# Four graph layers on one core: a first LSTM turn with orders of its own, and its loads rearranged

## The reference

```
h = relu(adj @ (x @ Wg0 + bg0))
h = relu(adj @ (h @ Wg1 + bg1))
for p in 1, 2, 3, 4:          # windows of p rows
    wins = h[:, :nw*p].reshape(B*nw, p, H)
    last = lstm_last(Wih[p-1], Whh[p-1], bih[p-1], bhh[p-1], wins)   # gates i, f, g, o
    h[:, p-1::p] = last       # the last row of each window is replaced
```

## Time and profile before

| what | us |
|---|---|
| median of 3 runs | 1201.16 (1200.19 to 1201.65) |
| the profiled execution | 1202.18 |
| its span | 1200.4 |
| PE busy | 1161.4 (97%) |
| DVE busy | 991.0 (83%) |
| ACT busy | 817.9 (68%) |
| POOL busy | 387.9 (32%) |

### The profile page before, as it was taken

One profiled execution on the slowest core, in us unless ns is written; L12 is line 12 of the kernel. 1 busy time (PEld: TensorE's weight loads), 2 busy tenths in 40 slices (PEclk: granted clock), 3 DMA queues, 4 the chain that ended last, 5 costly groups with the idle time before them and its releaser, 6 DMA issues. The chain is left out here.

```text
span 1200.4 us, 23784 instructions
## 1 busy us (share of the span) xinstructions
PE 1161.4 (97%) x7820; PEld 1021.9 (85%) x7820; DVE 991.0 (83%) x2791; ACT 817.9 (68%) x1826; POOL 387.9 (32%) x717
## 2 busy tenths in 40 slices
PE   5999999999999999999998999989999999999998
PEld 4798898998988989889897898877777798889997
DVE  5888988888889888898886899988877689976665
ACT  4685886868868768588685777757777777753332
POOL 4211100100001001010011677756666487742332
PEclk9999999999999999999998999999999999999999
DMA  9400000000000000000000000000000000002222
GB/s 261 121 1 1 1 2 0 0 0 0 0 0 0 0 0 0 0 0 0 1 1 1 2 2 2 2 1 1 2 1 1 1 2 1 2 3 69 71 69 73
DMA packets 26306, 20.85 MB, mean 17 GB/s; under 512 B 1776, under 2 KB 22256, under 8 KB 26224
## 3 DMA queue, kind: packets, MB, share of 16 engines
q1 hardware_dynamic: 25648, 19.68, 5.8%
q10 hardware_dynamic: 576, 0.13, 0.1%
HBM read 11.42 MB, written 8.39 MB: 17 GB/s over the span
## 5 line engine op out<-in xcount | busy, mean ns | idle before, releaser
L554 ACT ACTIVATE gate<-ps,b_lstm 128x256 f32<-128x256 f32 (+2 forms) x624 | 309.5, 564 | 94.4 <-PE ps L581 92.9
L579 PE MATMUL ps<-H_hi,w_hi 128*128 128x256 f32 (+2 forms) x624 | 210.3, 338 | 1.9 <-DVE H_lo L470 1.2
L580 PE MATMUL ps<-H_hi,w_lo 128*128 128x256 f32 (+2 forms) x624 | 205.1, 330 | 0.0
L581 PE MATMUL ps<-H_lo,w_hi 128*128 128x256 f32 (+2 forms) x624 | 193.2, 330 | 0.0
L131 POOL TENSOR_SCALAR rstd<-mv 128x8 f32<-128x8 f32 x16 | 5.0, 311 | 500.3 <-DVE mv L111 500.1
L579 PEld LDWEIGHTS ps<-H_hi,w_hi 128*128 128x128 f32 x624 | 117.7, 189 | 15.8 <-DVE H_lo L470 3.2
L580 PEld LDWEIGHTS ps<-H_hi,w_lo 128*128 128x128 f32 x624 | 117.9, 189 | 8.1
L581 PEld LDWEIGHTS ps<-H_lo,w_hi 128*128 128x128 f32 x624 | 115.4, 189 | 10.1 <-DVE H_lo L508 1.5
L579 PE MATMUL ps<-hid_hi,w_hi 128*128 128x256 f32 (+2 forms) x384 | 120.5, 320 | 0.3
L580 PE MATMUL ps<-hid_hi,w_lo 128*128 128x256 f32 (+2 forms) x384 | 116.8, 311 | 0.0
L561 ACT ACTIVATE tanh_c<-cell 128x512 f32<-128x512 f32 (+2 forms) x176 | 90.9, 516 | 24.5 <-DVE cell L498 17.4
(11 more groups left out here) (205 smaller groups left out, 3095.6 us busy)
## 6 DMA issues: line engine op xcount, KB each, us to landing
out<-x SPq DMA_DIRECT2D x32, 256.0 KB, 2.3
x<-in_WihT SPq DMA_DIRECT2D x1, 768.0 KB, 11.3
x<-in_WhhT SPq DMA_DIRECT2D x1, 768.0 KB, 6.0
x<-in_x_in SPq DMA_DIRECT2D x2, 256.0 KB, 3.6
x<-in_x_in SPq DMA_DIRECT2D x1, 512.0 KB, 7.9
x<-in_WihT SPq DMA_DIRECT2D x1, 256.0 KB, 8.2
tanh_c<-in_WqkvT SPq DMA_DIRECT2D x1, 192.0 KB, 5.0
w_sb<-in_W SPq DMA_DIRECT2D x1, 192.0 KB, 4.2
```

What stands on the lines that cost most here:

```text
L554: nc.scalar.activation(gate[:, g, z, 0:w * GB], gate_bank(g, k, m)[:, 0:w * GB], ACT.Tanh if z == G else ACT.Sigmoid, bias=b_lstm[:, 4 * ( ...
L579: nc.tensor.matmul(dst, w_hi[:, src, p - 1, z], v_hi, start=start, stop=False)
L580: return nc.tensor.matmul(dst, w_lo[:, src, p - 1, z], v_hi, start=False, stop=False)
L581: return nc.tensor.matmul(dst, w_hi[:, src, p - 1, z], v_lo, start=False, stop=stop)
```

## The change

The first turn gets orders of its own (FIRST_TENSOR, FIRST_VECTOR, FIRST_SCALAR). In them a letter x stands for the next item of a list of preparations of that engine, so that preparation can stand anywhere. The function `merged` runs the first order, then turns 1 to 7 as before.

- **Norm.** Statistics come in four quarters (SUMS 0 to 3), each with the addition of epsilon on DVE; POOL does the power only; DVE multiplies (SHIFT). ACT normalizes batch by batch, and PE waits for each batch of A0, not for four.
- **Loads.** Group 1 of x comes in two halves, directly behind group 0; the graph weights and the second bias are issued from ACT's queue, the edge lists and the LSTM biases from SP's behind x. SP then waits for the last quarter of the first 16 batches and issues the two 768 KB loads, and only then the second 16 batches of x.
- **Scratch.** Keys, edge rows and the attention operands move to a part of x that is loaded last but two; that load waits until they are taken.
- **Weights.** ACT splits weights 0 to 2 before its first A1 part, the other four and `w2` between gates later on. POOL makes the `w_lo` before `adj_causal`.
- **PSUM.** The sorting product and the fused weights both use bank 7; the fused one waits for the gate that reads this bank, and steps 1 and 2 of group 1 wait until they are taken.

```diff
+        PREPARE_TENSOR = [(COLUMN_SUM, 0), (BIAS_SUM, 0), (SORTED, 0), (FUSED, 0)]
+        PREPARE_VECTOR = [(SUMS, 0), (BIAS, 0), (SUMS, 1), (SHIFT, 0), (SUMS, 2), (SHIFT, 1), (SUMS, 3), (SHIFT, 2),
+                          (SHIFT, 3), (ADDEND, 0), (KEYS, 0), (LSTM_BIAS, 0), (RANK, 0), (RANK, 1), (MOVE, 0), (MOVE, 1),
+                          (DIAGONAL, 0), (TAKE_SORTED, 0), (TAKE_FUSED, 0)]
+        PREPARE_SCALAR = ([(NORM, j) for j in range(NB)] + [(SPLIT, n) for n in range(len(SPLITS))] + [(SPLIT2, 0)])
+
+
+        FIRST_TENSOR = ("xxaaaaabbabbaabbaaabbaaabbxbbbbaaxaaaaaaaabbabbbbbaaabbbbaaaaaaaaabaabbbbbabaaabbbabbbbbaaababb"
+                        "baaaaaaaaaabbabbbbbaaaabbbaaababbabaabbbbab")
+        FIRST_VECTOR = ("xxxxxxxxxxaxaxxxaabbxaabbxxattbbaaaxbaabbbaxtaabtbtaasbasabbasttaabbttbsbaassbaabsbsaabbaabbasa"
+                        "abbbbaabaabbaaabbabbaabbabb")
+        FIRST_SCALAR = ("xxxxxxxxaxaxxxxxxxbbxxxaaaaabbaxaaabbabbbbaaaabbxaaabbaabbaaaabbbbbaaaaxbbabxbaaabbbaabbaaaabbb"
+                        "babaaassbbabbsxaaatatabbbssbbssaaasbbbtbaabttttt")
...
+            for z in first_order:
+                if z == "x":
+                    prepare(*next(firsts[z]))
+                else:
+                    do(0, int(z in "bt"), *next(firsts[z]), False)
...
-                for to, s in ((w_g[:, 0], Wg0), (w_g[:, 1], Wg1), (b1_bc[:], bg1.to_broadcast([P, P]))):
-                    sp.dma_start(to, s).then_inc(S["ld_g"], 16)
-                sp.dma_start(*batches(GB, NB)).then_inc(S["ld_xb"], 16)
+                sp.dma_start(*batches(GB, GB + GB // 2)).then_inc(S["ld_xb"], 16)
+                sp.dma_start(*batches(GB + GB // 2, NB)).then_inc(S["ld_xc"], 16)
                 sp.dma_start(raw_all[0][:, 0:4 * P], WihT[:, 0:4 * P]).then_inc(S["ld_w1"], 16)
+                for to, s in ((ends_row, src_row.to_broadcast([P, E])), (ends_col[:, 0], src_col),
+                              (ends_col[:, 1], dst_col), (b_ih[:], bihT), (b_hh[:], bhhT)):
+                    sp.dma_start(to, s).then_inc(S["ld_ends"], 16)
+                sp.wait_ge(S["ld_xc"], 16)
+                for to, s in ((raw_all[0][:, 4 * P:], WihT[:, 4 * P:]), (raw_all[1][:, 4 * P:], WhhT[:, 4 * P:])):
+                    sp.dma_start(to, s).then_inc(S["ld_lstm"], 16)
                 sp.dma_start(*batches(NB, 2 * NB)).then_inc(S["ld_x1"], 16)
-                for to, s in ((raw_all[0][:, 4 * P:], WihT[:, 4 * P:]), (raw_all[1][:, 4 * P:], WhhT[:, 4 * P:]),
-                              (b_ih[:], bihT), (b_hh[:], bhhT)):
-                    sp.dma_start(to, s).then_inc(S["ld_lstm"], 16)
...
+                    if i * NB == SCRATCH:
+                        sp.wait_ge(S["o_taken"], 3)
...
-                for n, (g, j0, j1) in enumerate(((0, 0, GB // 2), (0, GB // 2, GB), (1, GB, NB))):
-                    r, sh = rstd[:, j0:j1], shift[:, j0:j1]
-                    pool.wait_ge(sa(g, "a_aggr"), j1 - g * GB)
-                    nc.gpsimd.tensor_scalar(r, mv[:, j0:j1, 1], EPS, None, ALU.add).then_inc(S["o_scale"], 1)
-                    nc.gpsimd.tensor_scalar(sh, mv[:, j0:j1, 0], -1.0, None, ALU.mult).then_inc(S["o_scale"], 1)
-                    pool.wait_ge(S["o_scale"], 3 * n + 2)
-                    nc.gpsimd.tensor_tensor(r, r, half[:, 0:j1 - j0], ALU.pow).then_inc(S["o_scale"], 1)
-                    pool.wait_ge(S["o_scale"], 3 * n + 3)
-                    nc.gpsimd.tensor_tensor(sh, sh, r, ALU.mult).then_inc(S["o_shift"], 1)
-
+                for n in range(NB // CB):
+                    r = rstd[:, n * CB:(n + 1) * CB]
+                    pool.wait_ge(S["o_eps"], n + 1)
+                    nc.gpsimd.tensor_tensor(r, r, half[:, 0:CB], ALU.pow).then_inc(S["o_pow"], 1)
+
+                for k, (src, p) in enumerate(SPLITS):
+                    pool.wait_ge(S["w_high"], k + 1)
+                    nc.gpsimd.tensor_tensor(w_lo[:, src, p], raw_of(src, p), w_hi[:, src, p].bitcast(F32),
+                                            ALU.subtract).then_inc(S["w_low"], 1)
...
+                def prepare(what, c):
+                    of = slice(c * CB, (c + 1) * CB)
+                    if what == SUMS:
+                        g, half_of = c * CB // GB, c * CB % GB
+                        dve.wait_ge(S[("ld_x0", "ld_xa", "ld_xb", "ld_xc")[c]], 16)
+                        norm_stats(g * GB, half_of, CB, sa(g, "a_stats"), g * GB)
+                        wait_apart(dve, sa(g, "a_stats"), half_of + CB)
+                        norm_aggr(c * CB, CB, sa(g, "a_aggr"))
+                        wait_apart(dve, sa(g, "a_aggr"), half_of + CB)
+                        nc.vector.tensor_scalar(rstd[:, of], mv[:, of, 1], EPS, None, ALU.add).then_inc(S["o_eps"], 1)
+                    elif what == SHIFT:
+                        dve.wait_ge(S["o_pow"], c + 1)
+                        nc.vector.scalar_tensor_tensor(shift[:, of], mv[:, of, 0], -1.0, rstd[:, of],
+                                                       ALU.mult, ALU.mult).then_inc(S["o_shift"], 1)
...
+                act.dma_start(b0_col[:], bg0).then_inc(S["ld_b0"], 16)
+                for to, s in ((w_g[:, 0], Wg0), (w_g[:, 1], Wg1)):
+                    act.dma_start(to, s).then_inc(S["ld_g"], 16)
+                act.dma_start(b1_bc[:], bg1.to_broadcast([P, P])).then_inc(S["ld_b1"], 16)
+
+                def prepare(what, n):
+                    if what == NORM:
+                        if n % CB == 0:
+                            act.wait_ge(S["o_shift"], n // CB + 1)
+                        relu_norm(act, 0, n // GB, n % GB, 1)
+                    elif what == SPLIT:
+                        src, p = SPLITS[n]
+                        act.wait_ge(*((S["ld_lstm"], n_lstm) if n else (S["ld_w1"], 16)))
+                        nc.scalar.activation(w_hi[:, src, p], raw_of(src, p), ACT.Copy).then_inc(S["w_high"], 1)
...
+                    elif what == FUSED:
+                        pe.wait_ge(S["ld_w"], n_w)
+                        pe.wait_ge(sa(1, "a_gate"), gates_before[1] + 1)
+                        nc.tensor.matmul(ps[:, 7, 0:P], wqkvT[:, 0], wqkvT[:, 1], start=True, stop=True)
+                        nc.tensor.matmul(ps[:, 7, P:2 * P], wqkvT[:, 2], wo_sb, start=True, stop=True).then_inc(
+                            S["o_products"], 1)
+
+                def part(i, g, what, k, m, before):
                     if opening(i) and (what, k, g) == (W0, 1, 1):
                         pe.wait_ge(S["o_bias"], 3)
                     if opening(i) and what in (SHARE, HIGH):
                         pe.wait_ge(S["w_low"], splits_of(steps[k][0]))
-                    if opening(i) and (what, k) == (HIGH, 1):
-                        pe.wait_ge(S["o_taken"], 3 if g else 1)
+                    if opening(i) and (what, k, g) == (HIGH, 1, 1):
+                        pe.wait_ge(S["o_taken"], 1)
+                    if opening(i) and (what, k, g) == (HIGH, 2, 1):
+                        pe.wait_ge(S["o_taken"], 3)
...
-                        pe.wait_ge(sa(g, "a_hn"), i * GB + (k + 1) * CB)
+                            pe.wait_ge(sa(g, "a_hn"), i * GB + (k + 1) * CB)
                         for b in range(CB):
+                            if not before:
+                                pe.wait_ge(sa(g, "a_hn"), k * CB + b + 1)
                             ins = nc.tensor.matmul(ps[:, 4 * g + k, b * T:(b + 1) * T],
                                                    hn[:, g * GB + k * CB + b], adjT_sb[:], start=True, stop=True)
```

More of the change, by code:

```diff
@@ L196, in four_layers @@
         ones_r = hid_lo[:, 0, 0:P]
[L197 to L200, removed]
+        SCRATCH = RAW - NB
+        scratch = x[:, SCRATCH:RAW, :].rearrange("p b c -> p (b c)")
+        key_row, is_less, ends_rowf = (scratch[:, k * E:(k + 1) * E] for k in range(3))
+        ends_row = scratch[:, 3 * E:4 * E].bitcast(I32)
+        wqkvT = scratch[:, 4 * E:4 * E + 3 * P].rearrange("p (k c) -> p k c", k=3)
+        wo_sb, adj_diag = (scratch[:, 4 * E + k * P:4 * E + (k + 1) * P] for k in (3, 4))
         steps = []
@@ L422, in move_to_rank @@
[L422 to L426, removed]
-                def part(i, g, what, k, m, before):
-                    if opening(i) and (what, k, g) == (U1, 0, 0):
+                def prepare(what, c):
[12 more added lines that the diff above has]
+                                                       ALU.mult, ALU.mult).then_inc(S["o_shift"], 1)
+                    elif what == BIAS:
+                        dve.wait_ge(S["o_products"], 1)
+                        dve.wait_ge(S["ld_b0"], 16)
+                        nc.vector.tensor_scalar(b0_part[:], ps[:, 7, 0:P], b0_col[:, 0:1], None, ALU.mult).then_inc(
+                            S["o_bias"], 1)
+                        nc.vector.tensor_scalar(cut0[:], ps[:, 7, 0:P], b0_col[:, 0:1], -1.0, ALU.mult,
+                                                ALU.mult).then_inc(S["o_bias"], 1)
+                    elif what == KEYS:
```

(35 more changed lines are left out.)

121 lines of the change are left out of this document (34 added, 87 removed).

## The result

| | before | changed |
|---|---|---|
| median | 1201.51 (20 runs, 1198.61 to 1203.48) | 1199.29 (20 runs, 1196.50 to 1202.16) |
| profiled execution, its span | 1202.18, 1200.4 | 1199.86, 1197.9 |
| first LSTM product | 32.92 | 26.20 |
| mark M: first H_lo eviction of turn 1 | 111.55 | 107.71 |

What follows compares the result with a forecast made beforehand. TensorE (PE), busy 1161.4 us of 1200.4, was taken as the bound. 8.50 + 0.28 - 0.4 - 0.4 = 8.0, less 2.0 for POOL's subtractions, gave 6.0 us gained and 1195.2 us; range 1192.3 to 1199.3.

Steps and rivals of the forecast that it cites:

- What can be taken out: Opening of the first turn, up to 44.40: PE's waits and half clock work there could give 8.50 us.
- walk: Step-by-step timing of the first turn's new order: first LSTM product at 26.1, HIGH of step 3 8.0 us ahead.
- Parts 1 to 3: Opening: PE's first product 0.28 us earlier net, new x landings harmless, LSTM weights landed at 17 at no cost.
- the step that the prediction called harmless: Loads of group 1's x: landing early, about 7.5 and 8.5, or late, 11.7 for the last, does no harm.
- C: Rival, chance 0.07: LSTM weights land near 29, first LSTM product near 32.5, no gain, 1199.5 to 1201 us.
- Part 4: New order of the first turn: every input in time, PE 8.0 us ahead at HIGH of step 3.
- Part 5: LSTM steps of the first turn: four POOL subtractions cost DVE 4 us, PE half, 2.0; five `hn` cost 0.
- Rival A: LSTM steps, chance 0.20: four subtractions cost DVE 1.25 us each, all 5.0 lands on PE, gain 3.0, time 1198.2.
- No later stretch of the span is touched: Behind the first turn: orders of turns 1 to 8 and the later layers are the same; no change counted.

Runs made afterwards that it cites:

- low_set_only: The changed kernel with POOL only setting the low halves of weight splits 3 to 6 to zero, not subtracting: 1194.19 us, ratio 0.9948 to the kernel before.
- splits_early: The changed kernel with ACT's weight splits 3 to 6 moved ahead, so POOL subtracts all seven between 21 and 30: 1195.40 us, ratio 0.9957 to the kernel before.
- no_wait: The changed kernel without SP's wait for the last quarter of x ahead of the two LSTM loads: 1198.69 us, ratio 0.9975 to the kernel before.
- ends_late: The changed kernel with the five small loads issued after SP's wait for the last quarter of x: 1197.91 us, ratio 0.9972 to the kernel before.
- splits_ends: The changed kernel with the edits of splits_early and ends_late together: 1194.16 us, ratio 0.9929 to the kernel before.
- best: The changed kernel with the edits of splits_ends and the four unread products of warm3_before: 1190.90 us, ratio 0.9911 to the kernel before.
- control_before: The kernel before, unedited, run against itself: ratio 1.0002.
- warm_after: The changed kernel with two unread 512-column products before the last transposes of layer 1: 1196.25 us, ratio 0.9957 to the kernel before.
- warm3_before: The kernel before with four unread products, two before layer 1's last transposes, one each at PE's end of layers 2 and 3: 1198.40 us, ratio 0.9973.
- warm3_after: The changed kernel with the same four unread products as warm3_before: 1195.49 us, ratio 0.9943 to the kernel before.

## Why the prediction was wrong, by its steps

**What can be taken out: right, the 26.1 with luck.** The 3.47 stand and the half clock stretch are gone, and the first LSTM product came at 26.20 for a walk's 26.1. In the six profiles with this opening it came at 24.48 to 27.02, depending on when the clock rose: the four W0 halves took 1.98 us in low_set_only, 2.42 here and 3.62 in splits_early. So the walk had the middle and this profile happened to lie there.

**Parts 1 to 3: right in sum by two errors.** The third quarter of x came at 10.09, not 7.5 to 8.2, and PE waited 1.73 us for it; the early chunks after that ran at 0.9, not 0.98, and W0 at nearly full clock. The wait needs two things. One is the step that the prediction called harmless: it asked only whether a late quarter holds its own shifts, and missed that shift 1, for x long landed, stands behind SUMS 2 on DVE. Putting SHIFT1 first is the plain cure, and was not run. The other is the late landing. The five small loads that the change put on SP's queue behind x, which the prediction gave no cost, are its likely cause: six profiles against three say so, no_wait's against it, so it is not shown. Without the wait the first LSTM product came at 23.85 to 25.16 (ends_late, splits_ends, best), 1.4 us sooner in the mean than in the six. The weights were never late (C falls).

**Part 4: right within 0.5.** Without POOL's reads nearly all of the walk's 8.0 us is there: 6.7 at the first product (32.92 to 26.20) and behind it 78.63 - 77.57 = 1.1 (low_set_only) or 0.9 (splits_early), 7.6 to 7.8 in all. One sign was badly chosen: the first eviction of turn 1, forecast at 93 to 94, came at 97.39, only 2.05 before the old one, since the five `hn` of Part 5 (2.06 us) stand ahead of it on ACT. They cost PE next to nothing, as forecast: M is 3.84 ahead.

**Part 5: the step that failed.** "1.0 of DVE time each, 4 in all" was right: the four steps lost 1.1, 1.1, 1.0 and 1.0. "And half of it on PE, since the walk's slack holds the other half: 2.0 us" was wrong: it was 3.7 to 3.9 (81.5 less 77.8 and 77.6). The slack of 0.2 to 1.5 was that of one hand-off at a time. DVE's steps form one strict order in which the other group's next step stands behind the held one, so that a loss of 1.0 goes through to the step with the least slack (the four starts under low_set_only), and from 44.5 to 98 DVE is busy 49.57 us of 53.5 (fourth time in the row), where it was 48.04 of 55 in the earlier trace rows:

```profile
44.50:98.00 53.50, 51.67 (x339) 47.22 (x338) 49.57 (x121) 41.42 (x97) 13.70 (x18) 1.00 0.22 60
```

That is not the held time alone: low_set_only, which holds none of the four, has 46.73 of 50.8 in the same part (41.6 to 92.4). The plainest case is the first: `H` held 1.1 us, then CELL, then `srt`, for which PE waited 1.45 where the walk had 0.2. Rival A had the mechanism, with a size of 5.0 that is 1.2 too large as my 2.0 is 1.8 too small; that its time, 1198.2, lies near the measured one is in part the next term's doing. The page "SBUF — State Buffer" of the Trainium skill, section "Who interferes with whom", makes this very distinction, that the GpSimd instruction must read SBUF: low_set_only, where it only writes, agrees, with 0 of 4 steps held. I should have given A the larger chance: the `moved` row had shown the price on DVE, and 48.04 of 55 how little room there was for it.

**Behind the first turn: a term that was put at nothing.** "No later stretch of the span is touched" is true of the instructions and false of the clock. Both kernels fall to half clock where a layer ends, but not both each time. The profiled execution before:

```profile
650.30:660.30 10.00, 8.18 (x30) 6.38 (x31) 4.35 (x20) 1.79 (x3) 4.99 (x12) 0.50 0.00 0
...
799.00:815.00 16.00, 10.89 (x68) 9.10 (x67) 11.46 (x42) 7.74 (x20) 6.46 (x13) 1.00 0.00 1
```

and the changed one:

```profile
647.00:653.40 6.40, 4.66 (x16) 2.84 (x15) 3.74 (x18) 1.20 (x2) 2.85 (x7) 0.50 0.00 0
800.50:807.30 6.80, 6.23 (x22) 5.74 (x23) 3.03 (x11) 1.25 (x3) 3.88 (x6) 0.50 0.00 1
```

Before: 8.18 us of work at half clock, which is 4.1 us more than at full clock, and none near 800. Changed: half of 4.66 and of 6.23, 2.3 and 3.1. That is 1.3 us more, as much as is lost behind M (3.84 - 2.5, the difference of the spans). But the sum comes out so in part by luck. From M to the end the two kernels take 1088.8 and 1090.2 us here, and 1085.1 and 1085.9 with the four products and no half clock: if the products themselves cost nothing, the half clock stretches are worth 3.7 and 4.3, so 0.6 of the loss, and 0.75 is lost without any. The waits of PE there are the same in both (2.30 us for `H`, 1.05 at the layer's end), just 4 us earlier. Which stretch falls is not decided by the kernel's own text: control_before, the same kernel as before, had those near 650, 805 and 950, and the profile above only the first. In the medians the term is 3.84 - 2.2 = 1.6 us by this pair of profiles, or 3.5 - 2.2 = 1.3 by the means of three. The changed kernel has no half clock in the opening (1.7 us less), and yet its mean clock is 0.994 as before: what it saves there it spends later. What decides it run by run stays open, and so does what takes the other 0.75: with the four products the medians still lie 2.9 apart, not 3.5 to 4.25.

In all: the 8.0 was 7.6 to 7.8, the 2.0 was 3.7 to 3.9, and 1.3 to 1.6 went behind the turn, which had been put at nothing. That leaves 2.2 within these bounds.

## What to carry to other kernels

A GpSimd instruction that read on-chip memory beside a dense run of VectorE steps with two on-chip inputs cost VectorE nearly its own length each time (1.0 to 1.1 us for 1.25); where VectorE is busy 90%, count all of it on the critical engine, and put such instructions where VectorE reads from PSUM. A new load order and a new instruction order are one change: here the loads alone lost. Within a strict order, do not put a step whose input is there behind one whose input may be late. When a gain of some us is to be measured, ask which idle places later in the kernel lead to half clock; four products that nobody reads were worth 3.4 us on the kernel before and 3.8 on the changed one.

## What the runs showed of the hardware

- A 1.3 us subtraction on POOL held a VectorE step for 1.0 to 1.1 us; a 0.53 us memset in the same place held none (after, low_set_only). Three of POOL's own were stretched too, to 1.5, 1.5 and 1.96.
- PE fell to 1.2 GHz (granted clock 0.5) for 3.4 to 10.2 us at layer ends. At the first the fall came 0.2 us before the end of a wait of 2.30 us (before) and 0.6 us behind it (changed). With two 512-column products in the first of these waits its clock stayed in three profiles (warm_after, warm3_before, warm3_after) and fell for 3.4 us in a fourth (best).
- With five small loads in the queue behind x, SP's wait for x's last quarter ended at 10.2 to 10.9 (six profiles), without them at 8.9 to 9.5 (three). That they are the cause is not shown: no_wait had its third quarter early with them in place.
